# Inverse square roots as a power on GpSimd, mask added by VectorE, maximum subtracted by GpSimd, in a six-layer local-attention block

## What is computed

```
xs = shift_tokens(x)                      # second half of channels one token later
q, k, v = split(xs @ Wqkv)                # 16 heads of 64
q = l2norm(q) * q_scale;  k = l2norm(k) * k_scale;  rotary on both
sim = q k' * 8 over windows of 32 tokens, keys of the window and the one before, masked
x = x + (softmax(sim) @ v) @ Wo
h = shift_tokens(x); xn = (h - mean) / sqrt(var + 1e-5) * g + b
x = x + (a * gelu(gate)) @ W2,   a, gate = split(xn @ W1 + b1)
```

## Time and profile before

| what | us |
|---|---|
| median of 3 runs (lowest, highest) | 1910.44 (1904.49, 1916.37) |
| the profiled execution | 1909.64 |
| its span, first to last instruction | 1907.8 |
| busy PE / DVE / ACT / POOL | 1716.4 / 1468.1 / 1095.4 / 1088.4 |
| end of batch 0 (start of the first L914) | 196.80 |
| end of batch 43 | 1806.12 |
| start of the last L914 | 1898.81 |

### The profile page before, as it was taken

The page is one execution under the profiler, slowest core; times in us unless marked ns, Lnnn a source line. Parts: engine busy times, 40 slices in busy tenths (PEclk is TensorE's granted clock), DMA queues, the critical chain, the costliest instruction groups (busy, mean ns, idle before and its releaser), DMA issues.

```text
span 1907.8 us, 75895 instructions
## 1 busy us (share of the span) xinstructions
PE 1716.4 (90%) x30558; PEld 1209.9 (63%) x30558; DVE 1468.1 (77%) x2727; ACT 1095.4 (57%) x2035; POOL 1088.4 (57%) x970
## 2 busy tenths in 40 slices
PE   5689999999989999999999998999998999999986
PEld 2356666666666666666666666666666666666664
DVE  4688787878877877877887887777887888787764
ACT  2255665656655565656656665656665566566653
POOL 0366665556656655655666666565655655665540
PEclk9699999999999999999999999999999999999999
DMA  2122223222222322222322222222222232222222
GB/s 97 29 78 63 55 57 77 64 66 71 58 48 72 77 69 49 69 57 57 78 63 67 65 62 55 77 64 69 66 55 55 67 77 65 71 58 56 53 54 67
DMA packets 82897, 122.09 MB, mean 64 GB/s; under 512 B 25168, under 2 KB 28752, under 8 KB 82256
## 3 DMA queue, kind: packets, MB, share of 16 engines
q1 hardware_dynamic: 82512, 116.84, 24.4%
HBM read 20.28 MB, written 2.10 MB: 12 GB/s over the span
## 4 chain that ended last, share of the span: by engine, by line
PE 57%; ACT 15%; issue 15%; DVE 11%; ACTq 1%; DMA 0%; DVEq 0%; SPq 0%
PE QKb L450 12%; PE F L573 10%; PE O L510 9%; PE S L498 6%; PE VTb L473 5%; PE S L450 4%; ACT L665 3%; ACT E L665 3%; PE F L596 3%; ACT v_tok L676 3%; PE F L597 2%; PE S L521 2%; PE S L491 2%; ACT KT L659 2%; DVE hid L904 2%
## 5 line engine op out<-in xcount | busy, mean ns | idle before, releaser
L975 POOL TENSOR_TENSOR t<-t 128x512 f32<-128x512 f32 x384 | 488.2, 1271 | 426.1 <-DVE t L835 425.8
L835 DVE TENSOR_TENSOR t<-QKb,table 128x1024 f32<-128x1024 f32 x384 | 469.2, 1222 | 285.0 <-ACT sq L650 281.1
L969 POOL TENSOR_TENSOR t<-t,rn 128x512 f32<-128x512 f32 x384 | 413.7, 1077 | 178.0 <-DVE rn L896 170.9
L450 PE MATMUL QKb<-wq_sb,x_sh 128*128 128x512 f32 x768 | 413.3, 620 | 60.9 <-DVE t L835 51.8
L650 ACT ACTIVATE sq<-QKb 128x512 f32<-128x512 f32 x384 | 229.1, 597 | 332.9 <-PE QKb L450 332.8
L473 PEld LDWEIGHTS VTb<-cst,t 128*128 128x128 f32 x1536 | 193.7, 142 | 204.1 <-issue 202.3
L960 POOL TENSOR_TENSOR E<-E,rs 128x512 f32<-128x512 f32 x192 | 200.2, 1043 | 159.9 <-DVE rs L868 159.9
L510 PE MATMUL O<-PT,V 64*64 64x32 f32 x12288 | 232.2, 221 | 39.6 <-issue 38.1
L682 ACT COPY OT<-O 128x512 f32<-128x512 f32 x192 | 112.5, 586 | 263.8 <-PE O L510 263.8
L510 PEld LDWEIGHTS O<-PT,V 64*64 64x64 f32 x12288 | 205.9, 135 | 62.4 <-issue 43.7
L473 PE MATMUL VTb<-cst,t 128*128 128x128 f32 x1536 | 232.6, 274 | 0.3 <-issue 0.3
(11 more groups left out here) (136 smaller groups left out, 2197.5 us busy)
## 6 DMA issues: line engine op xcount, KB each, us to landing
V<-v_tok SPq DMA_DIRECT2D x1440, 64.0 KB, 2.0
wq_sb<-in_wqkv SPq DMA_DIRECT2D x36, 256.0 KB, 3.1
wo_sb<-in_wo SPq DMA_DIRECT2D x6, 512.0 KB, 3.6
w_sb<-in_w SPq DMA_DIRECT2D x6, 341.0 KB
w_sb<-in_w SPq DMA_DIRECT2D x6, 192.0 KB
y_spill<-OT SPq DMA_DIRECT2D x1, 1024.0 KB, 4.8
V<-y_spill SPq DMA_DIRECT2D x1, 1024.0 KB, 8.0
out<-V SPq DMA_DIRECT2D x4, 256.0 KB, 2.9
```

The lines of the kernel that those rows point to most:

```text
L450: return pe.matmul(out_, x_sh[:, pr, P * tile:P * (tile + 1)], wq_sb[:, col:col + 512], start=True, stop=True)
L835: dve.tensor_tensor(t12[:, v, :, :].rearrange("p c (h d) -> p c h d", h=8), QK_ps.rearrange("p (h d) -> p h d", h=8).unsqueeze(1) .to_broa ...
L969: pool.tensor_tensor(w, w, rn[:, vv // 4, 8 * (vv % 4):8 * (vv % 4 + 1)].unsqueeze(2) .to_broadcast([P, 8, DH]), ALU.mult).then_inc(qk_nor ...
L975: pool.tensor_tensor(w, w, t12[:, v, 1, :].rearrange("p (h c d) -> p h c d", h=8, c=2)[:, :, ::-1, :], ALU.add).then_inc(add_done, 1)
```

## The change

- `newton` goes. POOL computes the inverse roots: a floor and a power with exponent -0.5 on 128x32, after its other work of slots 5 and 1 and ahead of the add; and for the layer norm a power on 128x2 and the diagonal, first in slot 5 (lag F_DIAG 29). `var` and `rstd` are tiles of their own.
- PE writes no mask into the S banks. DVE adds the mask from `cst` while it copies S to E, then takes the maximum from E; POOL subtracts it one slot later (L_SUB); exp, norm, PT and PV run one to two slots later than before.
- The affine step moves from DVE to ACT, an activation with scale and bias, a slot after the scaling.
- Lags of the feed-forward part shift by two or three slots. On PE, the waits of PV and S come ahead of the transposes, W1 chunk 2 comes before PT, BC after WO, the second scan product before V; on ACT, the square of the centred rows, gelu 2 and the shifted copies stand at other places of the slot; on DVE the second scan addition stands ahead of t12.

```diff
-L_SS, L_NEWTON, L_SCALE, L_TR = 2, 5, 6, 7
+L_SS, L_RN, L_SCALE, L_TR = 2, 5, 6, 7
 L_V = 6
-L_S, L_EXP, L_NORM, L_PT, L_PV = 11, 12, 13, 14, 15
-F_WO, F_MID, F_MEAN, F_CENT, F_SQ, F_VAR, F_VCOPY, F_NEWTON = 19, 23, 25, 26, 26, 26, 27, 29
-F_BC, F_XN, F_W1, F_GEL, F_HID, F_W2, F_END = 30, 31, 31, 32, 33, 34, 35
+L_S, L_SUB, L_EXP, L_NORM, L_PT, L_PV = 11, 12, 13, 14, 16, 17
+F_WO, F_MID, F_MEAN, F_CENT, F_SQ, F_VAR, F_VCOPY, F_DIAG = 21, 25, 27, 28, 28, 28, 29, 29
+F_BC, F_XN, F_AFF, F_W1, F_GEL, F_HID, F_W2, F_END = 29, 31, 32, 34, 34, 35, 36, 37
 LEAD = 6
-RSQRT_SEED = float(0x5F1FFFF9)
-NEWTON = ((0.703952253, 0.703952253 * 2.38924456), (0.5, 1.5))
 C_ID, C_MASK, C_TAB = 0, P, P + 4 * KEYS
...
-ss = sb("ss", [P, 2, NORMS + NT])
-rn = sb("rn", [P, 2, NORMS + NT])
-nwt = sb("nwt", [P, NORMS + NT])
+ss = sb("ss", [P, 2, NORMS])
+rn = sb("rn", [P, 2, NORMS])
+minus_half = sb("minus_half", [P, NORMS])
+var = sb("var", [P, NT])
+rstd = sb("rstd", [P, NT])
 QT = sb("QT", [P, 2, HP, N])
...
+            a, k, st, pr = quad(s, par, v, L_PV)
+            if live(a, QUADS):
+                if k == 0:
+                    for c in range(4):
+                        wait(pe, v_moved[c], moved(st + 1, c))
+                wait(pe, pt_evac, a + 1)
+                wait(pe, o_evac, a)
+            a, k, st, pr = quad(s, par, v, L_S)
+            if live(a, QUADS):
+                if k % 2 == 0:
+                    wait(pe, tr_evac, st * SLOTS + 4 * (k // 2 + 1))
...
-                for p in range(2):
-                    pe.matmul(S2[:, p, 0:4 * KEYS], ident_bf[:, :], mask_bf[:, :], start=True, stop=False,
-                              skip_group_check=True)
                 for ct in range(4):
                     hp, tile = 2 * k + ct // 2, ct % 2
                     for w in range(WPT):
...
-                                           start=False, stop=ct == 3, skip_group_check=True)
+                                           start=True, stop=True)
...
+            f, pr = batch(s, par, v, F_HID)
+            if f is not None:
+                ff_w1(f, pr, [2])
...
             if live(a, QUADS):
                 wait(pe, p_norm, a + 1)
-                wait(pe, sub_done, upto(a + 2, QUADS))
+                wait(pe, mask_done, s_units(s, v))
                 for ct in range(4):
...
             u, vv, st, pr = unit(s, par, v, L_V)
             if live(u, UNITS) and vv % 2 == 0:
                 if vv < 4 and pr == 0:
                     wait(pe, in_v[c], 16 * (st // B + 1))
                 wait(pe, v_evac, v_units(st, vv, 0) - 1)
-                wait(pe, sub_done, s_units(s, v))
+                wait(pe, mask_done, s_units(s, v))
                 project(V_ps, pr, c // 2, V_COLS[c % 2]).then_inc(v_ready, 1)
-            recurrence(in_fill(s, v, 1))
...
+            if f is not None:
+                wait(pe, diag_done, f + 1)
+                wait(pe, ff_final, f)
+                pe.matmul(BANK_BC[:, 0:N], ones[:, :], diag[:, :, :].rearrange("p t q -> p (t q)"),
+                          start=True, stop=True).then_inc(bc_ready, 1)
...
+            f, pr = batch(s, par, v, F_HID)
+            if f is not None:
+                gelus(f, pr, [2])
...
                 act.copy(v_tok[:, c // 2, 512 * (c % 2):512 * (c % 2 + 1)], V_ps).then_inc(v_evac, 1)
+            f, pr = batch(s, par, v, F_MID)
+            if f is not None:
+                wait(act, mid_done, f + 1)
+                act.copy(xs[0:64, :], xm[0:64, pr, :]).then_inc(xs_done, 1)
...
                 stage(s + 1, 1 - par)
+            f, pr = batch(s, par, v, F_AFF)
+            if f is not None:
+                if pr == 0:
+                    wait(act, in_ffn, (f // B + 1) * 48)
+                wait(act, xr_done, f + 1)
+                act.activation(xc[:, :], xc[:, :], ACT.Identity, bias=prm[:, R_B:R_B + 1],
...
-            f, pr = batch(s, par, v, F_HID)
-            if f is not None:
-                gelus(f, pr, [2])
...
                 finish(f, pr)
-            f, pr = batch(s, par, v, F_BC)
-            if f is not None:
-                rstd = rn[:, LN_HALF, NORMS:].unsqueeze(2).to_broadcast([P, NT, P])
-                wait(dve, nw_seq, ln_newton_count(f))
...
                 dve.tensor_tensor(xc[:, :], xc[:, :], BANK_BC[:, 0:N], ALU.mult).then_inc(xr_done, 1)
-                if pr == 0:
-                    wait(dve, in_ffn, (f // B + 1) * 48)
-                wait(dve, xr_done, f + 1)
-                dve.tensor_scalar(xc[:, :], xc[:, :], prm[:, R_G:R_G + 1], prm[:, R_B:R_B + 1],
-                                  ALU.mult, ALU.add).then_inc(xn_done, 1)
+            recurrence(in_fill(s, v, 1))
             f, pr = batch(s, par, v, F_VCOPY)
             if f is not None:
                 wait(dve, var_ready, f + 1)
-                dve.tensor_scalar(ss[:, LN_HALF, NORMS:], BANK_VAR[:, 0:NT], 1e-5, None, ALU.add)\
+                wait(dve, rstd_done, f)
+                dve.tensor_scalar(var[:, :], BANK_VAR[:, 0:NT], 1e-5, None, ALU.add)\
                    .then_inc(var_copied, 1)
...
                 wait(dve, sq_done, u + 2)
+                if vv % 4 == 0:
+                    wait(dve, rn_done, rn_count(st - 1, vv // 4))
                 dve.tensor_reduce(ss[:, vv // 4, 8 * (vv % 4):8 * (vv % 4) + 16],
...
                 wait(dve, s_ready, a + 1)
                 Sv = S2[:, :, 0:4 * KEYS].rearrange("p b (c k) -> p b c k", k=KEYS)
-                mv_ = mx[:, k, :].rearrange("p (b c) -> p b c", b=2)
-                dve.tensor_reduce(mv_, Sv, AX_X, ALU.max).then_inc(max_done, 1)
-                wait(dve, max_done, a + 1)
+                Ek = E[:, k, :].rearrange("p (c b k) -> p b c k", c=4, b=2)
                 wait(dve, pt_ready, a - 3)
                 if isinstance(a, int) and a == 0:
                     wait(dve, yT_done, 4)
-                dve.tensor_tensor(E[:, k, :].rearrange("p (c b k) -> p b c k", c=4, b=2), Sv,
-                                  mv_.unsqueeze(3).to_broadcast([P, 2, 4, KEYS]),
-                                  ALU.subtract).then_inc(sub_done, 1)
+                dve.tensor_tensor(Ek, Sv, cst[:, C_MASK:C_MASK + 4 * KEYS]
+                                  .rearrange("p (c k) -> p c k", k=KEYS).unsqueeze(1)
+                                  .to_broadcast([P, 2, 4, KEYS]), ALU.add).then_inc(mask_done, 1)
+                wait(dve, mask_done, a + 1)
+                wait(dve, sub_done, a - 3)
+                dve.tensor_reduce(mx[:, k, :], E[:, k, :].rearrange("p (c k) -> p c k", k=KEYS), AX_X, ALU.max)\
+                   .then_inc(max_done, 1)
             a, k, st, pr = quad(s, par, v, L_EXP)
             if live(a, QUADS):
                 wait(dve, exp_done, a + 1)
                 wait(dve, sum_done, a + 1)
                 wait(dve, p_norm, a - 3)
                 dve.reciprocal(rs[:, k, :], sm[:, k, :]).then_inc(rs_done, 1)
-            recurrence(in_fill(s, v, 1))
-            u, vv, st, pr = unit(s, par, v, L_NEWTON)
-            f, _ = batch(s, par, v, F_NEWTON)
-            if vv % 4 == 0 and (live(u, UNITS) or f is not None):
-                newton(st, vv // 4, u, f)
-    def newton(st, half, u, f):
...
     def hidden(f, par, chunks):
...
+            f, pr = batch(s, par, v, F_DIAG)
+            if f is not None:
+                wait(pool, var_copied, f + 1)
+                pool.tensor_tensor(rstd[:, :], var[:, :], minus_half[:, 0:NT], ALU.pow).then_inc(rstd_done, 1)
+                wait(pool, rstd_done, f + 1)
+                pool.tensor_tensor(diag[:, :, :], ident.unsqueeze(1).to_broadcast([P, NT, P]),
+                                   rstd[:, :].unsqueeze(2).to_broadcast([P, NT, P]),
+                                   ALU.mult).then_inc(diag_done, 1)
             a, k, st, pr = quad(s, par, v, L_NORM)
             if live(a, QUADS):
                 wait(pool, rs_done, a + 1)
                 pool.tensor_tensor(w, w, rs[:, k, :].unsqueeze(2).to_broadcast([P, 8, KEYS]),
                                    ALU.mult).then_inc(p_norm, 1)
+            u, vv, st, pr = unit(s, par, v, L_RN)
+            if live(u, UNITS) and vv % 4 == 0:
+                wait(pool, ss_done, upto(st * (SLOTS // 2) + 2 * (vv // 4) + 2, UNITS // 2))
             u, vv, st, pr = unit(s, par, v, L_SCALE)
             if live(u, UNITS):
                 if vv % 4 == 0:
-                    wait(pool, nw_seq, newton_count(st, vv // 4))
+                    wait(pool, rn_done, rn_count(st, vv // 4))
                 wait(pool, add_done, u + 1)
                 w = t12[:, vv, 0, :].rearrange("p (h d) -> p h d", h=8)
                 pool.tensor_tensor(w, w, rn[:, vv // 4, 8 * (vv % 4):8 * (vv % 4 + 1)].unsqueeze(2)
                                    .to_broadcast([P, 8, DH]), ALU.mult).then_inc(qk_norm, 1)
+            a, k, st, pr = quad(s, par, v, L_SUB)
+            if live(a, QUADS):
+                wait(pool, max_done, a + 1)
+                w = E[:, k, :].rearrange("p (c k) -> p c k", k=KEYS)
```

(26 more changed lines are left out.)

74 lines of the change are left out of this document (21 added, 53 removed).

## The result

| | before | after |
|---|---|---|
| median of runs on the same chip (4 each) | 1907.78 | 2127.93 (2119.78 to 2136.22) |
| ratio to before, 95% interval | | 1.115 (1.108 to 1.121) |
| profiled execution / its span | 1909.64 / 1907.8 | 2123.79 / 2121.9 |
| mean step, batch 0 to 43 | 37.43 | 42.19 |

A forecast was written before the change was run, and what follows sets the result against it. Bound taken as PE in slots 3 to 7 and an ACT and DVE path in slots 0 to 2. From 1909.6, steps -147, fill -7, drain +2 give 1757 us; range 1725 to 1795, for 8 in 10 1722 to 1865.

The forecast's parts named there:

- GpSimd: POOL's work per step: 27.9 us plus two 128x32 powers taken at 0.8 each, so 29.5, under PE's step.
- Rival (b): POOL becomes the bound through the 128x32 powers in slots 1 and 5, break-even 4.8 us each; over 1% slower, chance 0.12.
- What queues behind POOL's new waits: POOL's queue in slots 1 and 5: powers of 0.8 just covered; uncovered, each costs what it is above 1.3.
- Slot lengths: PE's eight dense slots of a step after the change, 3.35 to 4.64 us each, sum 32.4.
- Mean step: A step of eight slots: 32.4 plus issue waits 1.3 plus restarts 0.3, 34.0 us; bounds 33.4 and 35.1.
- Mask: Two bf16 matmuls before each S leave PE's path: 4 x 0.22 = 0.9 us a step gained, 0.5 at the low end.
- DVE and ACT: Work per step: DVE falls from 29.7 to about 25 us, ACT rises from 22.5 to about 25.6.
- Fill and drain: Outside the 43 equal steps: fill -7 us (between -25 and +8), drain +2 (between -6 and +12).
- Table switches: Four ACT table switches a step instead of two, 1.283 us each, all covered with 0.2 to 0.4 to spare.
- rival (d): A table switch between a PE result and a waiting gelu costs twice its row: step 37.5, time 1908; chance 0.05.
- Rival (a): A path over ACT and DVE stays: step 35 to 37 us, time 1800 to 1886, likeliest 1825; chance 0.20.
- Rival (c): No gain: PE's issue waits grow to 4 us a step, filling what is freed; 1886 and up; chance 0.02.

The follow-up runs named there:

- the quarters: Changed kernel with each pair of powers cut in four of 16 columns, one per odd slot: 2049.99; with the subtraction also on DVE: 1897.32.

## Why the prediction was wrong

**The step that failed: the size of a power, in the part "GpSimd".** I took 0.8 between 0.15 and 2.4 and it measured 5.46. The lower end came from a product and the upper one from DVE's eight operations times 1.5; neither row held a power, and I let the upper end stand as if it were a bound. The Trainium skill (GPSIMD Engine Reference, 3.1) gave no better: by its 12 cycles an element for data-dependent branches I had estimated 0.3. The rest of that sum came out right, 27.9 + 2 x 5.46 = 38.8 where POOL works 38.71, with some luck, since three small terms were low (0.71 and twice 0.29, for 0.15 each).

**Rival (b) happened**, with its chance of 0.12. It priced the step by POOL's sum alone: 38.8, 1.4 over the 37.43 of before, with the break-even at p = 4.8. The step is 4.8 over. So a second step failed: the limits of 3.0 and 4.8 for p come from the sum, although the part "What queues behind POOL's new waits" had another price, that uncovered each power costs what it is above 1.3. With 5.46 that gives a step of 34.0 + 2 x 4.16 = 42.3, and 42.19 was measured; by it the break-even with 37.43 is at p = 3.0, not 4.8. I had the path and didn't use it for the rival.

The close agreement is partly luck. With half the columns (2.93) the same rule gives 37.3, and the mean step is 35.29. From there to the whole power a step grows by 6.90 for 5.06 more of powers, 1.4 for 1, where a fixed circle or POOL's sum would give 1. PE's clock is 1.00 in 35 of the 43 steps of the one kernel and 0.84 to 0.96 in all of the other, but what it adds isn't isolated. That POOL's sum doesn't decide while scale and power stand close is shown by the kernel with the subtraction on DVE (a step of 42.00 with 34.8 of POOL), and that it does once they are cut and drawn apart by the quarters.

**Right, as the kernel without a power shows.** *Slot lengths*: 32.4 forecast, 32.40 measured, PE at 100%. *Mean step*: 34.0 forecast, 1443.44 / 43 = 33.57. *Mask*: 0.9, with 0.5 as the low end, measured 0.84 a step. *DVE and ACT*: 25 and 25.6 forecast, 25.4 and 25.7 measured (25.8 and 26.1 in after). *Fill and drain*: -7 and +2 forecast, -13.0 (41.90 to 183.77 is 141.87) and -11.0 (81.65 for 92.69); the drain lies below its range of -6 to +12, and so it does in after (-8.7). The forecast without POOL's power would have been 38 too high, half of it in the steps: PE's waits for issue were 29.4 us in the 43 steps, 0.7 a step, where I had 1.3.

**Table switches**: covered, as forecast, while PE is the bound; rival (d) falls, since removing all four gives back at most 0.7 of 5.1 a step in the three kernels where it was tried, and nothing in two of them. **Rival (a)** was wrong for this kernel and right for the one with Newton on DVE: there a path over t12 is left, 36.0 a step in the mean, in its range of 35 to 37. **Rival (c)** fell with the kernel without a power.

**Newton**: its removal from DVE was forecast to free t12. It does; with the eight operations kept, the new structure is at 1836.12, and they cost it 1836 - 1718 = 118 us. That is 2.45 between the mean steps (36.02 - 33.57), against 8.6 for the power (42.19 - 33.57). 1836.12 is the best time here that computes everything. PE's wait for t12 accounts for 1.6 of the 2.45; the rest was not isolated.

**Open**: how much of after's loss is the clock's. PE's lower clock is seen in its windows and goes with the longer steps, but no run holds the waits and changes the clock, so which of the two makes the other isn't shown.

## What to carry to other kernels

A transcendental operation that no row shows isn't bounded by sums and products of the same shape; time that one operation by itself before a kernel is built around it, or write the range up to where the kernel breaks. Where an engine's queue holds a long operation that other engines need results from behind, follow the circle back to that operation, and compare its length with the step as well as the engine's sum: here, moving other work off the engine helped the sum alone and gained nothing, while cutting the operation and moving it away from its reader opened the circle. A price for a delay that is worked out in one part belongs in the rival's sum too. An order that keeps table switches under the bound's work is worth more than fewer switches.

## What the hardware showed that I hadn't expected

**GpSimd's power** goes by the column: 0.158 us for a column of 128 values, 0.4 fixed, against 0.254 in all for a product of 128x32. It hardly depends on what stands around it: 5.458 for 32 columns in after, 5.448 in the kernel before with the power, where 34 columns take 5.849.

**PE's clock.** Two short windows of after, around the wait that follows a power and behind it:

```profile
1238.00:1242.00 4.00, 1.09 (x55) 0.95 (x62) 1.22 (x1) 0.70 (x2) 4.00 (x5) 0.99 0.00 0
1242.00:1250.00 8.00, 8.00 (x111) 5.85 (x101) 3.23 (x5) 3.02 (x6) 6.29 (x6) 0.58 0.23 58
```

PE is busy 1.09 of 4.00 in the first; in the second it has work throughout and is granted 0.58 of full speed, mostly the lower level of 1.2 GHz. A wait of some 3 us is so followed by 8 in which PE does what would take 4.6 at full clock (8.00 x 0.58, an estimate). The step before has both kinds of wait: behind the one of 3.0 that ends at 1199.79 the clock is 0.64 up to 1204 and 0.53 from there to 1208; behind the one of 1.7 that ends at 1220.38 it stays at 1.00. Without a power the mean over the steps is 0.99, and with half the columns the step shown has 1.00. PE's own slack doesn't settle whether this costs anything: the two steps at 40.22, where POOL's sum decides, are equal with 1.00 and 0.92, while in after and with the subtraction on DVE, where PE is a part of the circle and also has slack (36.41 busy of 41.13), the steps with the lower clock are the longer ones.
